# A transformer tower on one core: the last halving of the weighted pixels and the normalisation of the aggregate move from VectorE to GpSimd

## The chip, the core and the metric

The kernel runs on one core of a Trainium2 chip. A core has five engines, each with its own queue of instructions: TensorE (PE, matrix products and transposes), VectorE (DVE), ScalarE (ACT), GpSimd (POOL) and SyncE (SP), which issues the transfers here. Engines run side by side and hand work over by semaphores. Data lies in SBUF (128 partitions), matrix products arrive in PSUM. GpSimd reads and writes SBUF only in this kernel. The metric is the time of one execution on the device, in microseconds (us).

## The reference

Input `x` is (128, 64, 64, 64) in fp32: 128 images with 64 channels of 64x64 pixels. Three layers follow one another; the change lies in the first, the tokenizer:

```python
s = conv_stride                                   # 4
hw, n, d = (h * w, s * s, c // num_heads)         # 256 tokens, 16 pixels each, 8 channels a head
x = features.reshape(b, c, h, s, w, s)
reduce_feats = x.mean((3, 5)).reshape(b, c, hw).transpose(0, 2, 1)
unf = x.transpose(0, 1, 2, 4, 3, 5).reshape(b, c, hw, n).transpose(0, 2, 3, 1)
q = _ln(reduce_feats, ln_q_w, ln_q_b) @ Wq.T
kv = _ln(unf, ln_kv_w, ln_kv_b) @ Wkv.T
...
attn = jax.nn.softmax(jnp.einsum('bhpd,bhpnd->bhpn', q * scale, k), axis=-1)
aggre = jnp.einsum('bhpn,bhpnd->bhpd', attn, v)
return reduce_feats + aggre @ proj_w.T + proj_b
```

Each token looks at its own 16 pixels: a softmax over them, per head, and the weighted sum of their values. Behind it come a linear attention in chunks of 128 tokens with decay, a layer norm, a mixture of 8 experts of which 2 are taken, and a second layer norm:

```python
h = _layernorm(h + _L0_attn_ref(h, ...), axis=-1)
h = _layernorm(h + _L0_ffn_ref(h, ...), axis=-1)
```

## The kernel before

The program has two blocks. The first does the tokenizer, the linear attention and the first layer norm, and leaves its result in SBUF (`h1`); the second does the experts and stores. The change touches the first block only.

The first block works in 128 units. A unit is 128 tokens of each of two images, so `[128, 128]` tiles hold 128 tokens by two times 64 channels. Every engine has a function `step(i, r)`; step 4i + r of each engine works on several units at once, each at another stage: `there(i, r, lag)` asks whether unit 4i + r - lag exists, and `done(i, r, lag, per)` is the count of a semaphore when that unit's stage is through (`per` counts a unit). So the order of the work on an engine is the order in which its `step` is written, and what an instruction waits for is written before it. `units` runs ten steps of straight code at the start, then a loop of 29 passes with four steps in its body, then ten steps of straight code at the end. In the text, "the first step" to "the fourth step" are those of the loop's body; the first stands behind the loop's jump.

What happens around the change, for a unit u:

- One step after its keys and values, VectorE makes the softmax weights `aw` (128 tokens by 16 pixels by 16 heads of the two images) and `rden`, the reciprocal of the sum of the exponentials, at the end of the step.
- In the next step GpSimd multiplies the values `vs` by the weights, four products of 128x512 (L699), and folds the 16 pixels to 8 by two additions of 128x512 (L706), each in place in `pv`. In its queue there follow two parts of the attention of an older unit, `qm` (L713) and `htok` (L719), and the pixel sums of a unit two steps ahead, from `xb` by `xt` to `red` (L729 to L737).
- VectorE, behind the key product of its first quarter (`keys(0)`, L816), sums the 8 pixels that remain to `agg` by one reduction (L859) whose input is read with a stride of 128 elements, and multiplies by `rden` into `aggn` (L863). Then comes `keys(1)`, then three small instructions of a Newton step (L871 to L873) that wait for ScalarE's `y0s`, then the scaling of the queries `q` (L878) and `keys(2)`.
- TensorE, behind its `keys(1)`, transposes `aggn` (`aggregated`, L491), makes the second half of the values (L407), projects the turned aggregate (`projected`, L496) and goes on with `keys(2)` (L380, L385). ScalarE, between the two, adds a bias to the turned aggregate (`aggT`, L647), behind the squares of the centred input (`sqs`, L563) on its queue.

The key products form a chain of their own: TensorE writes quarter j into one bank of PSUM, VectorE multiplies it by the queries (`kqs`), and only then may TensorE write quarter j + 1.

## Time and profile before

| | |
|---|---|
| time, median of 3 runs | 2807.53 us (2804.64 to 2809.35) |
| the profiled execution | 2810.09 us, its span 2808.4 us |
| mean granted TensorE clock | 0.957 of full speed |
| TensorE busy | 2357.4 us (84%) |
| VectorE busy | 2050.6 us (73%) |
| ScalarE busy | 1907.3 us (68%) |
| GpSimd busy | 1785.9 us (64%) |

The first block takes some 2350 us of the span, the second the rest. Busy shares are averages: they tell which engine has room, and not what a step waits for. For that there are the waits (which engine stood idle, in front of which instruction, until whose work had ended) and the timeline, which lists instructions in order of time. Ends of matrix products are modelled, and GpSimd's spans are rough. In the rows, L699 is line 699 of the kernel.

### The profile page before, as it was taken

Reading aid. Unit: us, or ns where it says so; the run is one execution under the profiler, and the core shown is the slowest. Engines: PE = TensorE matmul, PEld = TensorE weight load, DVE = VectorE, ACT = ScalarE, POOL = GpSimd, SP = SyncE. Lnnn points to the kernel's source line nnn. Section 1 sums busy time; section 2 is a strip of 40 time slices with the busy share of each in tenths; the row PEclk is TensorE's granted clock in tenths of the full one; section 3 lists DMA queues with packets and bytes.
Section 4 is the critical chain, followed back from the end, with each engine's and each line's share of the span. In section 5 each row is a group of like instructions: output and inputs, shape, how many; then the busy total and the mean of one; then the engine's idle time right before and its main releaser. Section 6 shows DMA issues by size and latency. Waiting matters only on the chain. (4 is left out here: it accounts for less than half of the span.)

```text
span 2808.4 us, 93560 instructions
## 1 busy us (share of the span) xinstructions
PE 2357.4 (84%) x32965; PEld 1125.1 (40%) x32965; DVE 2050.6 (73%) x4680; ACT 1907.3 (68%) x4717; POOL 1785.9 (64%) x1821
## 2 busy tenths in 40 slices
PE   2788888888888888888888888888888886999997
PEld 1344444444444444444444444444444443333332
DVE  4677777777777777777777777777777776888887
ACT  3777777777777777777777777777777773555554
POOL 3677777777777777777777777777777763222323
PEclk9899999999999999999999999999999997999999
DMA  5333333222233333333323222333333300001001
GB/s 88 62 62 62 62 62 62 60 58 57 58 62 62 62 62 62 62 62 62 62 62 61 58 58 57 62 61 61 62 62 62 62 17 1 16 19 22 19 19 27
DMA packets 573761, 148.58 MB, mean 53 GB/s; under 512 B 573440, under 2 KB 573440, under 8 KB 573440
## 3 DMA queue, kind: packets, MB, share of 16 engines
q1 hardware_dynamic: 573440, 143.52, 25.7%
q8 instruction: 297, 4.87, 0.7%
q14 instruction: 24, 0.20, 0.0%
HBM read 135.09 MB, written 8.39 MB: 51 GB/s over the span
## 5 line engine op out<-in xcount | busy, mean ns | idle before, releaser
L699 POOL TENSOR_TENSOR pv<-vs,aw 128x512 f32<-128x512 f32 x512 | 535.3, 1078 | 565.8 <-DVE aw L916 565.8
L581 ACT ACTIVATE xd<-xb 128x512 f32<-128x512 f32 x512 | 573.6, 1146 | 0.0
L380 PE MATMUL ps<-xb,w_ckv 64*64 64x512 f32 x2048 | 553.4, 617 | 2.4 <-ACT sqs L563 1.9
L385 PE MATMUL ps<-xb,w_ckv 64*64 64x512 f32 x2048 | 553.4, 617 | 0.0
L816 DVE TENSOR_TENSOR kqs<-ps,qqT 128x512 f32<-128x512 f32 x512 | 351.3, 686 | 233.4 <-PE ps L385 231.3
L827 DVE TENSOR_TENSOR sm<-ps,decay 128x1024 f32<-128x1024 f32 x256 | 301.5, 1220 | 212.4 <-PE ps L462 212.4
L563 ACT ACTIVATE sqs<-ps 128x512 f32<-128x512 f32 x512 | 305.1, 596 | 87.7 <-PE ps L385 87.7
L570 ACT ACTIVATE vs<-ps 128x1024 f32<-128x1024 f32 x256 | 262.4, 1025 | 115.3 <-PE ps L407 112.4
L729 POOL TENSOR_TENSOR xt<-xb 128x512 f32<-128x512 f32 x256 | 326.1, 1297 | 21.6 <-issue 21.2
L706 POOL TENSOR_TENSOR pv<-pv 128x512 f32<-128x512 f32 x256 | 320.5, 1274 | 0.0
L859 DVE TENSOR_REDUCE agg<-pv 128x128 f32<-128x1024 f32 x128 | 253.2, 1978 | 77.9 <-POOL pv L706 77.9
L407 PE MATMUL ps<-w_ckv,xd 64*64 64x64 f32 x16384 | 298.9, 222 | 0.1
L407 PEld LDWEIGHTS ps<-w_ckv,xd 64*64 64x64 f32 x16384 | 264.5, 135 | 39.5 <-issue 16.9
L346 PE MATMUL ps<-kqs,selk 128*32 128x512 f32 x1024 | 161.6, 708 | 135.9 <-issue 76.8
L1217 ACT ACTIVATE hid<-ps,b1p 128x1024 f32<-128x1024 f32 x128 | 142.7, 1115 | 164.8 <-PE ps L1118 164.6
L1318 DVE TENSOR_TENSOR hid<-ps,hid 128x512 f32<-128x512 f32 x256 | 163.7, 685 | 25.1 <-PE ps L1130 13.3
L462 PE MATMUL ps<-qm,kT 32*128 32x512 f32 x1024 | 171.4, 744 | 0.0
L732 POOL TENSOR_TENSOR xt<-xt 128x512 f32<-128x512 f32 x128 | 162.6, 1270 | 10.0
L713 POOL TENSOR_TENSOR qm<-qT,hm 128x512 f32<-128x512 f32 x128 | 133.6, 1044 | 43.7 <-ACT kT L598 43.7
L349 PE MATMUL ps<-sqs,selv 128*32 128x512 f32 x1024 | 159.7, 700 | 0.0
L597 ACT ACTIVATE qT<-ps 128x128 f32<-128x128 f32 x128 | 35.5, 278 | 170.1 <-PE ps L437 170.1
L475 PEld LDWEIGHTS ps<-sm,vpad 128*32 128x32 f32 x4096 | 104.1, 109 | 108.0 <-issue 101.5
(213 smaller groups left out, 4455.6 us busy)
## 6 DMA issues: line engine op xcount, KB each, us to landing
xb<-in_x_dram SPq DMA_DIRECT2D x512, 256.0 KB, 4.3
out_dram<-outb SPq DMA_DIRECT2D x128, 64.0 KB, 1.6
w1p<-in_L_ffn_w_dram SPq DMA_DIRECT2D x16, 16.0 KB
w2p<-in_L_ffn_w_dram SPq DMA_DIRECT2D x8, 16.0 KB
b1p<-in_L_ffn_b_dram SPq DMA_DIRECT2D x8, 0.2 KB
sm<-in_L_tok_Wkv_dram SPq DMA_DIRECT2D x4, 16.0 KB, 2.0
w_av<-in_L_attn_w_qkv_dram SPq DMA_DIRECT2D x4, 16.0 KB, 2.1
b2v<-in_L_ffn_b_dram SPq DMA_DIRECT2D x4, 2.0 KB
```

Source lines behind the costliest of these rows:

```text
L380: nc.tensor.matmul(KB[own, :], w_ckv[own, 2 * P + m * C:2 * P + (m + 1) * C], xv[own, j], start=True, stop=True)
L385: mm = nc.tensor.matmul(CB[(1 - m) * C:(2 - m) * C, :], w_ckv[own, m * C:(m + 1) * C], xv[own, j], start=True, stop=True)
L407: mm = nc.tensor.matmul(VB[m][h * C:(h + 1) * C, n * C:(n + 1) * C], xv[own, d, b, h * C:(h + 1) * C], w_ckv[own, P + m * C:P + (m + 1) * ...
L563: nc.scalar.activation(sqs[:, j, :], CB, ACT.Square).then_inc(cs_done, 1)
L570: nc.scalar.activation(vs[:, s, v * 8 * P:(v + 1) * 8 * P].rearrange("p (n m c) -> p m n c", m=2, c=C), ps[:, 2:4, :].rearrange("p m (n c) ...
L581: nc.scalar.activation(xd[:, j, :].rearrange("p (b t) -> p b t", b=ST), xb[:, f, :].rearrange("p (b t d) -> p d b t", b=ST, d=ST)[:, j], A ...
L699: nc.gpsimd.tensor_tensor(pv[:, at].rearrange("p (k d) -> p k d", d=D), vs[:, s, at].rearrange("p (k d) -> p k d", d=D), aw[:, j * W4:(j + ...
L706: nc.gpsimd.tensor_tensor(pv[:, j * 4 * P:(j + 1) * 4 * P], pv[:, j * 4 * P:(j + 1) * 4 * P], pv[:, (j + 2) * 4 * P:(j + 3) * 4 * P], ALU. ...
L729: ins = nc.gpsimd.tensor_tensor(xt[:, h * H:(h + 1) * H], xb[:, f, h * H:(h + 1) * H], xb[:, f, (h + 2) * H:(h + 3) * H], ALU.add)
L816: V.tensor_tensor(kqs[:, j, :].rearrange("p (t d) -> p t d", d=ST), KB.rearrange("p (t d) -> p t d", d=ST), qqT[:, s, :].unsqueeze(2).to_b ...
L827: V.tensor_tensor(sm[:, f * 1024:(f + 1) * 1024].rearrange("p (h c) -> p h c", c=P), ps[:, 2 * f:2 * f + 2, :].rearrange("p g (h c) -> p ( ...
L859: V.tensor_reduce(agg[:], pv[:, 0:8 * P].rearrange("p (n c) -> p c n", c=P), AX, ALU.add).then_inc(agg_ch, 1)
```

## The change

Three things. GpSimd makes a third addition of 128x512 behind its two, which folds 8 pixels to 4, under a new semaphore `pv_half`; `pv_done` now counts this one. VectorE's reduction reads 4 pixels (512 elements of a partition) in place of 8. The multiplication by `rden` leaves VectorE and stands on GpSimd, behind `htok` and ahead of the pixel sums, with the same two waits. Two waits are new on VectorE: the reduction waits until GpSimd has read the `agg` of the unit before, and the reciprocal waits until GpSimd has read `rden`.

```diff
--- before.py
+++ after.py
@@ -218,6 +218,7 @@
             ex_done = sem("ex_done")
             aw_done = sem("aw_done")
             pv_ch = sem("pv_ch")
+            pv_half = sem("pv_half")
             pv_done = sem("pv_done")
             agg_ch = sem("agg_ch")
             agg_done = sem("agg_done")
@@ -705,7 +706,10 @@
                             pool.wait_ge(pv_ch, done(i, r, 2, ST, j - 1))
                             nc.gpsimd.tensor_tensor(pv[:, j * 4 * P:(j + 1) * 4 * P], pv[:, j * 4 * P:(j + 1) * 4 * P],
                                                     pv[:, (j + 2) * 4 * P:(j + 3) * 4 * P],
-                                                    ALU.add).then_inc(pv_done, 1)
+                                                    ALU.add).then_inc(pv_half, 1)
+                        pool.wait_ge(pv_half, done(i, r, 2, 2))
+                        nc.gpsimd.tensor_tensor(pv[:, 0:4 * P], pv[:, 0:4 * P], pv[:, 4 * P:8 * P],
+                                                ALU.add).then_inc(pv_done, 1)
                     if there(i, r, 3):
 
                         pool.wait_ge(qk_ev, done(i, r, 3, 2))
@@ -718,6 +722,14 @@
                         pool.wait_ge(vk_ev, done(i, r, 3, 2))
                         nc.gpsimd.tensor_tensor(htok[:, o, :], htok[:, o, :], bp_row[:],
                                                 ALU.add).then_inc(hb_done, 1)
+                    if there(i, r, 2):
+
+                        pool.wait_ge(agg_ch, done(i, r, 2, 1))
+                        pool.wait_ge(agT_pe, done(i, r, 3, 1))
+                        nc.gpsimd.tensor_tensor(aggn[:].rearrange("p (j d) -> p j d", d=D),
+                                                agg[:].rearrange("p (j d) -> p j d", d=D),
+                                                rden[:].unsqueeze(2).to_broadcast([P, SL, D]),
+                                                ALU.mult).then_inc(agg_done, 1)
                     if there(i, r, -2):
 
                         f = (r + 2) % 4
@@ -855,14 +867,10 @@
                     keys(0)
                     if there(i, r, 2):
 
-                        dve.wait_ge(pv_done, done(i, r, 2, 2))
-                        V.tensor_reduce(agg[:], pv[:, 0:8 * P].rearrange("p (n c) -> p c n", c=P), AX,
+                        dve.wait_ge(pv_done, done(i, r, 2, 1))
+                        dve.wait_ge(agg_done, done(i, r, 3, 1))
+                        V.tensor_reduce(agg[:], pv[:, 0:4 * P].rearrange("p (n c) -> p c n", c=P), AX,
                                         ALU.add).then_inc(agg_ch, 1)
-                        dve.wait_ge(agg_ch, done(i, r, 2, 1))
-                        dve.wait_ge(agT_pe, done(i, r, 3, 1))
-                        V.tensor_tensor(aggn[:].rearrange("p (j d) -> p j d", d=D),
-                                        agg[:].rearrange("p (j d) -> p j d", d=D),
-                                        rden[:].unsqueeze(2).to_broadcast([P, SL, D]), ALU.mult).then_inc(agg_done, 1)
                     keys(1)
 
                     link, n = chain(dve, newt_ch, (4 * i + r + 2) * 3)
@@ -917,6 +925,7 @@
                                         ALU.mult).then_inc(aw_done, 1)
                         V.tensor_reduce(den[:], sn.rearrange("p n j -> p j n"), AX, ALU.add).then_inc(den_done, 1)
                         dve.wait_ge(den_done, done(i, r, 1, 1))
+                        dve.wait_ge(agg_done, done(i, r, 2, 1))
                         link(V.reciprocal(rden[:], den[:]))
                         assert n[0] == 5
                 units(dve, step)
```

GpSimd's queue, in the second step of the loop's body, from the products to the pixel sums; before:

```order
L699 TENSOR_TENSOR pv<-vs,aw 128x512 x4
L705 REGISTER_ALU
L706 TENSOR_TENSOR pv<-pv 128x512 x2
L712 REGISTER_ALU
L713 TENSOR_TENSOR qm<-qT,hm 128x512
L719 TENSOR_TENSOR htok<-htok,bp_row 128x128
L727 REGISTER_ALU
L729 TENSOR_TENSOR xt<-xb 128x512 x2
```

The same place in the changed kernel, whose lines lie further down (`hm` is the mask of the heads, REGISTER_ALU computes a count that is waited for):

```order
L700 TENSOR_TENSOR pv<-vs,aw 128x512 x4
L706 REGISTER_ALU
L707 TENSOR_TENSOR pv<-pv 128x512 x2
L711 TENSOR_TENSOR pv<-pv 128x512
L716 REGISTER_ALU
L717 TENSOR_TENSOR qm<-qT,hm 128x512
L723 TENSOR_TENSOR htok<-htok,bp_row 128x128
L729 TENSOR_TENSOR aggn<-agg,rden 128x128
L739 REGISTER_ALU
L741 TENSOR_TENSOR xt<-xb 128x512 x2
```

Everything behind the products has moved down by one instruction, and the pixel sums by two; `aggn` has `qm` and `htok` between itself and the addition on which it depends by way of VectorE.

VectorE's queue from `keys(0)` to the Newton step, again in the second step of the loop's body, before and then after, with the semaphores that each row waits for:

```order
L816 TENSOR_TENSOR kqs<-ps,qqT 128x512 [waits sel_pe,qq_done,kc_pe]
L859 TENSOR_REDUCE agg<-pv 128x128 [waits pv_done]
L863 TENSOR_TENSOR aggn<-agg,rden 128x128 [waits agT_pe,agg_ch]
L812 REGISTER_ALU
L816 TENSOR_TENSOR kqs<-ps,qqT 128x512 [waits kc_pe]
```

After:

```order
L828 TENSOR_TENSOR kqs<-ps,qqT 128x512 [waits sel_pe,qq_done,kc_pe]
L872 TENSOR_REDUCE agg<-pv 128x128 [waits agg_done,pv_done]
L824 REGISTER_ALU
L828 TENSOR_TENSOR kqs<-ps,qqT 128x512 [waits kc_pe]
L877 ISA
L879 SCALAR_TENSOR_TENSOR ps<-ps,y0s 128x16x3 [waits rs_ch]
```

One instruction is gone between the two key products, and the second follows the reduction. The queues of TensorE, ScalarE and SyncE are as they were.

## Rows read from the trace of the kernel before

**Rows 1.** The page: busy us, share of the span, instructions.
```profile
PE 2357.4 (84%) x32965; PEld 1125.1 (40%) x32965; DVE 2050.6 (73%) x4680; ACT 1907.3 (68%) x4717; POOL 1785.9 (64%) x1821
```
**Rows 2.** Groups by line: count, busy us, mean ns, idle us before and its releaser.
```profile
L699 POOL TENSOR_TENSOR pv<-vs,aw 128x512 f32<-128x512 f32 x512 | 535.3, 1078 | 565.8 <-DVE aw L916 565.8
...
L706 POOL TENSOR_TENSOR pv<-pv 128x512 f32<-128x512 f32 x256 | 320.5, 1274 | 0.0
...
L859 DVE TENSOR_REDUCE agg<-pv 128x128 f32<-128x1024 f32 x128 | 253.2, 1978 | 77.9 <-POOL pv L706 77.9
...
L719 POOL TENSOR_TENSOR htok<-htok,bp_row 128x128 f32<-128x128 f32 x128 | 58.8, 460 | 1.7
...
L1327 DVE TENSOR_REDUCE nst<-y 128x8 f32<-128x512 f32 x32 | 21.6, 676 | 5.0 <-POOL y L1052 5.0
...
L1286 DVE TENSOR_REDUCE top<-rest 128x8 f32<-128x64 f32 x32 | 7.0, 220 | 1.1
```
**Rows 3.** One line, the normalisation: duration in ns, least, median, greatest.
```profile
L863 DVE TENSOR_TENSOR aggn<-agg,rden x128: 291/746/1157, 86.6 to 2341.5; 128x128 f32<-128x128 f32 x128
```
**Rows 4.** Waits from 1000 to 1200 us: us in total, times, longest us.
```profile
PE ps L491 <- DVE aggn L863: 5.2, 9, 0.7
...
DVE ps L871 <- ACT y0s L642: 3.7, 8, 0.7
PE ps L496 <- ACT aggT L647: 3.4, 9, 0.4
...
PE ps L491 <- ACT l L556: 1.0, 2, 0.5
```
**Rows 5.** Timeline, a third step: start us, us, instruction, count [idle before, releaser].
```profile
1004.92 0.42 DVE L916 TENSOR_TENSOR aw<-ps,yrs 128x256 f32<-128x256 f32 x1
...
1005.50 4.18 POOL L699 TENSOR_TENSOR pv<-vs,aw 128x512 f32<-128x512 f32 x4 [3.92 <-DVE aw L916]
...
1009.64 2.52 POOL L706 TENSOR_TENSOR pv<-pv 128x512 f32<-128x512 f32 x2
...
1012.10 1.05 POOL L713 TENSOR_TENSOR qm<-qT,hm 128x512 f32<-128x512 f32 x1
1012.19 1.97 DVE L859 TENSOR_REDUCE agg<-pv 128x128 f32<-128x1024 f32 x1 [0.70 <-POOL pv L706]
...
1013.10 0.47 POOL L719 TENSOR_TENSOR htok<-htok,bp_row 128x128 f32<-128x128 f32 x1
...
1014.20 0.75 DVE L863 TENSOR_TENSOR aggn<-agg,rden 128x128 f32<-128x128 f32 x1
...
1015.05 0.30 PE L491 MATMUL ps<-ident,aggn 128*128 128x128 f32 x1 [0.68 <-DVE aggn L863]
...
1015.28 1.16 PE L407 MATMUL ps<-w_ckv,xd 64*64 64x64 f32 x64
...
1016.04 0.36 ACT L647 ACTIVATE aggT<-ps,bv_col 128x128 f32<-128x128 f32 x1
...
1016.43 1.22 DVE L878 TENSOR_SCALAR q<-qps,yrs 128x64 f32<-128x64 f32 x2
...
1016.55 0.46 PE L496 MATMUL ps<-aggT,w_pj 128*128 128x128 f32 x2
...
1018.10 0.69 DVE L816 TENSOR_TENSOR kqs<-ps,qqT 128x512 f32<-128x512 f32 x1 [0.45 <-PE ps L385]
```
**Rows 6.** Timeline, the first step behind the jump.
```profile
1049.32 1.97 DVE L859 TENSOR_REDUCE agg<-pv 128x128 f32<-128x1024 f32 x1
...
1051.04 1.27 POOL L732 TENSOR_TENSOR xt<-xt 128x512 f32<-128x512 f32 x1
...
1051.33 1.13 DVE L863 TENSOR_TENSOR aggn<-agg,rden 128x128 f32<-128x128 f32 x1
...
1054.38 0.46 PE L496 MATMUL ps<-aggT,w_pj 128*128 128x128 f32 x2 [0.40 <-ACT aggT L647]
```
**Rows 7.** Timeline of TensorE, a fourth step.
```profile
1031.77 0.30 PE L491 MATMUL ps<-ident,aggn 128*128 128x128 f32 x1 [0.47 <-DVE aggn L863]
...
1033.49 0.46 PE L496 MATMUL ps<-aggT,w_pj 128*128 128x128 f32 x2 [0.32 <-ACT aggT L647]
```

## The prediction

> **What bounds the kernel now.** I read the busy shares first. No engine is full: TensorE is busy 84% of the span, VectorE 73%, GpSimd 64% [rows 1]. So the shares don't decide it, and the question is which wait ends last around the aggregate. The groups by line come next: VectorE's reduction of eight pixels takes 1.98 us, 128 times [rows 2], and its normalisation 0.29 to 1.16 us, median 0.75 [rows 3]. That is 2.7 us of VectorE in each step, and it looks like much. The waits of a steady stretch correct this [rows 4]: of 11 steps, TensorE's transpose of the aggregate waits for VectorE in 9 and for ScalarE in 2, but the projection two places later on the same queue waits again, for ScalarE, in 9.
>
> The timeline of one step, the third of the four in the loop's body, shows why [rows 5]. GpSimd multiplies from 1005.50 and adds to 1012.16. VectorE reduces from 1012.19 to 1014.17 and normalises to 1014.95, and TensorE transposes at 1015.05. The values follow until 1016.44. The projection starts at 1016.55. Its other input, `aggT`, was ready on ScalarE at 1016.40, and ScalarE had reached it late: it began at 1016.04, 0.69 behind the transpose's end, since queries, squares and the logarithm chain stand ahead of it on that queue. So ScalarE fixes the projection at 0.15 us behind `aggT`, and the aggregate only has to be in time. How much in time? Work that queues up on TensorE starts 0.07 us ahead of the modelled end of what precedes it (the values at 1015.28, the transpose's end at 1015.35), so the projection could have started at 1016.37: 0.18 us of slack. In the fourth step TensorE idles 0.32 us before the projection, in the first 0.40 [rows 6, 7], and over three steps of four 0.38 on average (3.4 us in 9 waits [rows 4]), so in the second like the first; with the same 0.07 the slack is 0.39, 0.47 and 0.47.
>
> **The change part by part.** Third addition on GpSimd: 128x512, as the two before it, 1.27 us [rows 2], behind a wait on GpSimd's own semaphore. In the third step it begins at about 12.24 (0.08 for that wait is my estimate) and ends at 13.51 (I write 12.24 for 1012.24). Behind it queue `qm` (1.05) and `htok` (0.47), which overlap their predecessor by 0.05 each: `qm` to 14.50, `htok` to 14.92 [rows 5]. Only then comes the new multiplication.
>
> Reduction of four pixels on VectorE: not in the trace. From below: the reduction of 512 adjacent elements took 0.68 us [rows 2]. From above: 1978 ns for 1024 is 0.76 more than the adjacent pace would give (a fixed 0.155 plus 1.02 ns an element, fitted through 512 elements and the 220 ns of 64 [rows 2]); if that surplus belongs to the 128 outputs and not to the elements, 512 cost 0.155 + 0.52 + 0.76 = 1.44 us. I take 1.07: fixed part 0.155, the rest halved, since the reads alone keep their stride. It then runs 13.54 to 14.61, and GpSimd hears of it 0.16 later (VectorE's `aw` ends at 5.34, GpSimd starts at 5.50 [rows 5]): 14.77. The multiplication isn't waiting for it, because its queue is busy until 14.92. That holds for any reduction up to 1.2 us.
>
> The normalisation on GpSimd: not in the trace either. Its nearest form is the 128x512 product with a broadcast factor, 1078 ns; `htok` (460 ns for 128) and the additions (1274 ns for 512) split into 189 ns fixed and 2.12 ns an element [rows 2]. A quarter of 889 plus 189 is 0.41. Bounds: 0.29, the shortest on VectorE [rows 3], and 0.46, `htok`. From 14.87 it ends at 15.28, and TensorE starts 0.10 later as before: 15.38 in place of 15.05. So the transpose is 0.33 late in the third step, 0.18 of it is slack, and 0.15 us is lost. In the fourth step the same sum (0.31 to 0.33 late, slack 0.39) gives nothing. In the second it was ScalarE that the transpose waited for [rows 4], so it is late by less than 0.33, with 0.47 of slack: nothing. In the first step GpSimd is early (VectorE reduces long after the additions, 1049.32 [rows 6]); the product is there by 1050.9, before the old one began, and the transpose could go earlier, but ScalarE's chain keeps the projection at 1054.38: no gain.
>
> Sum: the third step's pattern occurs 31 times (29 passes of the loop and two units outside): 31 x 0.15 = 4.6 us. In the last two units nothing covers the chain: 1.35 more for the addition (with its wait), 0.83 less for the reduction, and the product on GpSimd instead of VectorE with its signal, 0.3, make about 0.8 each; TensorE's other work hides most of the first, so 1.0. Together 5.6 us on a profiled execution of 2810.1 us. That one lies 2.6 above the median of the runs, 2807.5, and so the forecast is 2813.
>
> What VectorE gains, 1.98 - 1.07 + 0.75 = 1.66 us a step, I cost at nothing. The key product after it starts about 0.3 earlier, but then the Newton step waits for ScalarE's `y0s`, in 8 of 11 steps already before [rows 4].
>
> GpSimd gets 1.27 + 0.41 us a step more. Its sums of the next but one unit (`xt`, `red`) move by 1.7 us in three steps and by 2.4 in the first. It idles 4.4 us a step on average before the next weights (565.8 us in 128 waits [rows 2]), and 3.92 before this one [rows 5], and `red` is read only in the next step, so this is covered. The new wait of VectorE before the reciprocal asks for a product that was finished 6 us before.
>
> **A rule against the change.** VectorE's normalisation takes 0.75 us here and 1.13 where a GpSimd addition has just begun: 1051.33 to 1052.46, with the addition of 1051.04 ending at 1052.31 [rows 6], while its shortest is 0.29. It stands still until GpSimd's instruction ends. The Trainium skill, GPSIMD Engine Reference (Key points), says that GpSimd shares its SBUF interfaces with VectorE and that VectorE instructions with two SBUF inputs contend: the trace agrees. The same page (Engine selection) says not to put elementwise work on GpSimd, about twice as slow for two inputs. By that alone the move would lose; by this trace it replaces 0.75 with an estimated 0.41, since the contention goes with it. The Trainium skill, VectorE: DVE Perf Modes (the perf-mode tier table), gives a reduction one element a cycle, which would make the new one as short as the lower bound; the 1.98 us of the old one speak against it, and the sum would stay the same.
>
> **Rivals.** (1) Slower clearly: the reduction costs per output. Place: the product on GpSimd then waits for VectorE. Price at 1.44 us: third step 13.54 + 1.44 + 0.16 = 15.14, transpose 15.65, 0.60 late, 0.42 lost; fourth step 0.60 late, 0.21 lost; others nothing. 0.63 x 30 = 19 us, with the ends 2828. It decides from 1.2 us on. For it: the halving is only argued. Against it: the surplus goes with the one property that the adjacent reductions lack, the stride, which acts on every element read. A late signal or a slow start on GpSimd would act at the same place in the same way, with 0.1 us costing 3 us, and up to 6 once the fourth step is reached.
>
> (2) Collision: the scaling of the queries (`q`) is a VectorE instruction that today waits for GpSimd's addition, 1.22 us for the pair at 1016.43 [rows 5]. With GpSimd 1.7 us later it meets the two back-to-back additions from `xb`. The first goes through at their boundary at 16.5, the second may stand until 17.8. The next key product starts at 18.10 today, waiting for TensorE. So it costs nothing unless the second falls behind a further addition, to 19.1: then about 0.9 us in one kind of step, 26 us, 2834.
>
> (3) Faster: VectorE sets the pace by its key products, and 0.3 us a step come back in three steps of four: 96 x 0.26 = 25 us, 2782. Against it are the waits for ScalarE and TensorE named above. Smaller and likelier: the first step after the loop's jump varies by a microsecond from pass to pass, and another layout in time may take 0.2 us of it, 6 us.
>
> **How the numbers follow.** A run of this kernel can be told from no change at 0.2%, 5.6 us. The forecast, a small loss of 2 to 8 us, has 0.65; its own range is 2809 to 2816. Rival 1 with late signals has 0.20, rival 2 has 0.06, rival 3 with the jump 0.09. The forecast lies on the bound, so its chance splits: 0.43 within 0.2% and 0.22 slower. With the rivals: slower 0.47 (0.22 + 0.20 + 0.05), same 0.44, faster 0.09. The range reaches down to 2806, which leaves out most of rival 3, and up to 2828, the end of rival 1.
>
> **What would show it.** The transpose about 0.45 us behind `htok`'s end in the third step, and TensorE's wait before the projection gone there; the same wait down to under 0.1 in the fourth, untouched in the second. The reduction near 1.07 us. GpSimd's idle time before the weights down by 1.7 us a step. I am wrong if the reduction is over 1.2 us, if GpSimd starts the product later than `htok` lets it, or if the Newton step after the key product starts earlier than ScalarE's `y0s` allows today.

## The result, and the profile after

The changed kernel takes 2832.61 us (median of 4 runs, 2828.81 to 2833.62) against 2808.44 for the kernel before on the same chip: a ratio of 1.010, 95% interval 1.0072 to 1.0128. The forecast was 2813, its range 2806 to 2828, so the result lies 4.6 us outside. The profiled execution took 2828.81 us, its span 2827.1, which is 18.7 more than before.

The page of the kernel after, busy us of each engine, answers to [rows 1]:

```profile
PE 2346.5 (83%) x32965; PEld 1125.2 (40%) x32965; DVE 1875.7 (66%) x4552; ACT 1911.0 (68%) x4717; POOL 1986.0 (70%) x2077
```

VectorE has 175 us less, GpSimd 200 more. The groups by line of the same kernel answer to [rows 2, 3]:

```profile
L700 POOL TENSOR_TENSOR pv<-vs,aw 128x512 f32<-128x512 f32 x512 | 535.0, 1076 | 354.6 <-DVE aw L924 354.6
...
L872 DVE TENSOR_REDUCE agg<-pv 128x128 f32<-128x512 f32 x128 | 136.2, 1064 | 208.3 <-POOL pv L711 208.3
...
L711 POOL TENSOR_TENSOR pv<-pv 128x512 f32<-128x512 f32 x128 | 162.6, 1270 | 10.0
...
L729 POOL TENSOR_TENSOR aggn<-agg,rden 128x128 f32<-128x128 f32 x128 | 51.8, 404 | 33.7 <-DVE agg L872 33.7
```

The new operations cost what was forecast: the reduction 1.06 us (1.07), the product 0.40 (0.41), the addition 1.27, and GpSimd's idle time before the weights fell from 565.8 to 354.6 us, 1.65 a step (1.7). A third step of the kernel after, in the timeline, answers to [rows 5]; brackets are idle time before an instruction and its releaser:

```profile
1008.99 1.27 POOL L711 TENSOR_TENSOR pv<-pv 128x512 f32<-128x512 f32 x1
...
1010.29 1.06 DVE L872 TENSOR_REDUCE agg<-pv 128x128 f32<-128x512 f32 x1 [2.03 <-POOL pv L711]
...
1011.22 0.45 POOL L723 TENSOR_TENSOR htok<-htok,bp_row 128x128 f32<-128x128 f32 x1
...
1011.63 0.40 POOL L729 TENSOR_TENSOR aggn<-agg,rden 128x128 f32<-128x128 f32 x1
...
1012.14 0.30 PE L492 MATMUL ps<-ident,aggn 128*128 128x128 f32 x1 [1.05 <-POOL aggn L729]
...
1013.19 1.52 DVE L886 TENSOR_SCALAR q<-qps,yrs 128x64 f32<-128x64 f32 x2
...
1013.46 0.49 PE L497 MATMUL ps<-aggT,w_pj 128*128 128x128 f32 x2
...
1013.59 1.02 ACT L571 ACTIVATE vs<-ps 128x1024 f32<-128x1024 f32 x1 [0.42 <-PE ps L408]
...
1015.03 0.69 DVE L828 TENSOR_TENSOR kqs<-ps,qqT 128x512 f32<-128x512 f32 x1 [0.32 <-PE ps L386]
...
1016.23 0.30 PE L431 MATMUL ps<-ident,q 128*128 128x128 f32 x1 [0.85 <-DVE kqs L828]
```

The product stands right behind `htok`, TensorE's transpose 0.47 us behind `htok`'s end, and the projection follows the values directly. All this is as forecast. Two things are not, and the same step of the kernel before shows them:

```profile
1016.50 1.02 ACT L570 ACTIVATE vs<-ps 128x1024 f32<-128x1024 f32 x1
...
1019.14 0.30 PE L430 MATMUL ps<-ident,q 128*128 128x128 f32 x1 [0.69 <-DVE kqs L816]
```

ScalarE's copy of the values' second half (L571 after, L570 before) waits 0.42 us for TensorE, where before it followed `aggT` without a wait. TensorE turns the queries (L431, before L430) 2.77 us after the projection's start in place of 2.59, which is 0.18 us later. The waits of TensorE and ScalarE over the whole loop, 230 to 2240 us (us in total, times, longest), of before:

```profile
PE ps L346 <- issue: 76.8, 28, 3.1
PE ps L430 <- DVE kqs L816: 61.2, 113, 0.7
...
PE ps L496 <- ACT aggT L647: 31.6, 84, 0.4
...
ACT vs L570 <- PE ps L407: 97.2, 112, 0.9
```

and of after:

```profile
PE ps L347 <- issue: 76.3, 28, 3.2
PE ps L431 <- DVE kqs L828: 75.8, 113, 0.9
...
PE ps L497 <- ACT aggT L648: 19.6, 56, 0.4
...
ACT vs L571 <- PE ps L408: 116.6, 171, 0.9
```

The copy waits 59 times more, about once in each third and each fourth step, and the turning of the queries waits 14.6 us longer in sum. The projection lost its wait in 28 steps: these are the fourth ones, where the forecast had left it under 0.1 us.

I measured each step from projection to projection, mean over the loop; an interval bears the name of the step whose projection ends it. What an engine does behind a step's projection therefore falls into the next interval: the third step's copy of the values and its turning of the queries lie in the fourth interval. Third: 16.575 us before, 16.716 after. Fourth: 16.949 and 17.129. First, the one that holds the loop's jump: 21.018 and 20.293. Second: 17.011 and 17.008. With 29, 29, 28 and 28 of them the loop's part is +4.1, +5.2, -20.3 and -0.1 us; the units ahead of the steady part give +0.9 and those behind it +4.4; the second block gives +24.5. Up to rounding that makes the 18.7.

So two surprises outweigh everything that the forecast argued about. The first is the shorter first step. Each line is one such step: its start and end, its length, the busy time of PE, PEld, DVE, ACT and POOL, and then TensorE's granted clock as a share of full speed (0.84 in the first line), ahead of the DMA share. Of before:

```profile
1033.49:1054.38 20.89, 16.73 (x240) 7.58 (x241) 13.12 (x27) 12.85 (x34) 14.71 (x16) 0.84 0.27 53
1104.90:1126.03 21.13, 16.75 (x241) 7.60 (x241) 13.14 (x27) 12.87 (x34) 14.74 (x16) 0.84 0.25 53
```

and of after:

```profile
1030.58:1050.99 20.41, 15.70 (x242) 7.43 (x241) 11.58 (x26) 13.10 (x34) 16.49 (x17) 0.92 0.25 54
1101.84:1120.54 18.70, 14.05 (x240) 7.19 (x241) 11.68 (x26) 13.12 (x34) 15.96 (x17) 1.00 0.29 60
```

At 0.84 TensorE ran at the lower level (1.2 GHz) for (1 - 0.84) x 2 x 20.9 = 6.7 us of the step, at 0.92 for half of that, at 1.00 never; it fell after TensorE's idle time at the jump. Before, 26 of 28 passes were of the first kind; after, 4 were, 20 of the second kind and 4 of the third. In sum over the loop the lower level holds for 184 us before and 96 after, while TensorE's wait at the jump itself is the same (76.8 and 76.3 us).

The second surprise is in code that the change doesn't touch. VectorE in the second block, 2536 to 2542 us, after:

```profile
2538.34 0.17 DVE L1310 TENSOR_SCALAR top<-top 128x8 f32<-128x8 f32 x1 [2.59 <-issue]
2540.60 0.17 DVE L1311 TENSOR_SCALAR top<-top 128x8 f32<-128x8 f32 x1 [2.09 <-issue]
2540.81 0.23 DVE L1312 TENSOR_TENSOR ra<-ra,top 128x64 f32<-128x64 f32 x1
```

The same three in the kernel before:

```profile
2534.31 0.40 DVE L1301 TENSOR_SCALAR top<-top 128x8 f32<-128x8 f32 x1
2534.74 0.52 DVE L1302 TENSOR_SCALAR top<-top 128x8 f32<-128x8 f32 x1
2535.30 0.23 DVE L1303 TENSOR_TENSOR ra<-ra,top 128x64 f32<-128x64 f32 x1
```

They are the first instructions behind the jump of the second block's loop. "issue" means a wait for nothing that the profile shows. It occurs in all five passes that begin with the jump back, twice in each, 22.3 us in sum, and in the kernel before it never occurs. The pages' part on DMA queues counts the packets of the instruction queues (packets, MB, share); after:

```profile
q8 instruction: 292, 4.78, 0.7%
q14 instruction: 50, 0.41, 0.0%
```

and before:

```profile
q8 instruction: 297, 4.87, 0.7%
q14 instruction: 24, 0.20, 0.0%
```

One queue fetched twice as many packets.

The waits and the 24.5 us are not quite the same thing. In the eleven kernels below that have no such waits the second block takes 466.2 to 469.2 us, and this goes with its own time at the lower clock level (35.6 to 49.2 us) at about 0.2 us for each us. In the changed kernel that time is 78.1 us (before 35.9), with one stretch right after each of the five pairs of waits. By the same slope, extrapolated, some 8 us of the 24.5 come with the clock and 16 from the waits themselves; this split is my estimate.

The Trainium skill, Runtime: NRT & Kernel Launch (Instruction fetch mechanics), says that instructions are fetched in blocks of 256, that most engines hold two of them and TensorE more, and that a taken branch whose target is in neither forces a fetch before execution goes on. The change takes three instructions out of VectorE's program ahead of that loop: its 323 instructions start at number 963 before and at 960 after. If a block begins between the two, the loop lies in two blocks before and in three after. The following runs test that first.

### The profile page after: what moved, and what is told of

It is laid out like the page before. It is cut to its first block and busy times, and to the rows that moved or that the text cites. A ratio compares the mean times of both kernels' runs of the same rounds, so it can differ in the third digit from the quotient of the medians.

```text
span 2827.1 us, 93857 instructions
## 1 busy us (share of the span) xinstructions
PE 2346.5 (83%) x32965; PEld 1125.2 (40%) x32965; DVE 1875.7 (66%) x4552; ACT 1911.0 (68%) x4717; POOL 1986.0 (70%) x2077
## 5 line engine op out<-in xcount | busy, mean ns | idle before, releaser
L700 POOL TENSOR_TENSOR pv<-vs,aw 128x512 f32<-128x512 f32 x512 | 535.0, 1076 | 354.6 <-DVE aw L924 354.6
L571 ACT ACTIVATE vs<-ps 128x1024 f32<-128x1024 f32 x256 | 262.1, 1024 | 132.2 <-PE ps L408 132.2
L741 POOL TENSOR_TENSOR xt<-xb 128x512 f32<-128x512 f32 x256 | 319.7, 1269 | 21.5 <-issue 21.0
L707 POOL TENSOR_TENSOR pv<-pv 128x512 f32<-128x512 f32 x256 | 320.6, 1274 | 0.0
L872 DVE TENSOR_REDUCE agg<-pv 128x128 f32<-128x512 f32 x128 | 136.2, 1064 | 208.3 <-POOL pv L711 208.3
L347 PE MATMUL ps<-kqs,selk 128*32 128x512 f32 x1024 | 150.3, 660 | 134.2 <-issue 76.3
L711 POOL TENSOR_TENSOR pv<-pv 128x512 f32<-128x512 f32 x128 | 162.6, 1270 | 10.0
L463 PE MATMUL ps<-qm,kT 32*128 32x512 f32 x1024 | 161.0, 701 | 0.0
L1050 POOL TENSOR_TENSOR outb<-y,yrs 128x512 f32<-128x512 f32 x32 | 33.4, 1042 | 177.0 <-DVE yrs L1347 177.0
L1127 PE MATMUL ps<-tokT,w1p 64*128 64x512 f32 x512 | 150.0, 664 | 0.0
```

What stands on the lines that cost most here:

```text
L571: nc.scalar.activation(vs[:, s, v * 8 * P:(v + 1) * 8 * P].rearrange("p (n m c) -> p m n c", m=2, c=C), ps[:, 2:4, :].rearrange("p m (n c) ...
L700: nc.gpsimd.tensor_tensor(pv[:, at].rearrange("p (k d) -> p k d", d=D), vs[:, s, at].rearrange("p (k d) -> p k d", d=D), aw[:, j * W4:(j + ...
L707: nc.gpsimd.tensor_tensor(pv[:, j * 4 * P:(j + 1) * 4 * P], pv[:, j * 4 * P:(j + 1) * 4 * P], pv[:, (j + 2) * 4 * P:(j + 3) * 4 * P], ALU. ...
L741: ins = nc.gpsimd.tensor_tensor(xt[:, h * H:(h + 1) * H], xb[:, f, h * H:(h + 1) * H], xb[:, f, (h + 2) * H:(h + 3) * H], ALU.add)
L1127: mm = nc.tensor.matmul(UB[p % 2][:, m, :], w1p[h, p, :], tokT[h, (r + ahead) % 4, :], start=True, stop=True)
```

## The experiments

Each kernel was timed in rounds together with the kernel before, whose median was 2811.03 us beside e1 to e4, 2809.27 beside e5 to e8 and 2812.21 beside e9 to e12; the ratio compares within these rounds. The steps are the mean intervals as above; "low" is the time at the lower clock level in the loop, "second block" the time from the last transpose of an aggregate to the end (us). All of these come from one profiled execution. The last column has the mean granted clock of that execution and, behind it, the median over all executions of the kernel: where the two differ, as in e3, e4, e6 and e9, the profiled one is not typical in its low time.

| kernel | ratio (95%) | third | fourth | first | second step | low | second block | clock |
|---|---|---|---|---|---|---|---|---|
| before | 1 | 16.575 | 16.949 | 21.018 | 17.011 | 184 | 466.5 | 0.957, 0.956 |
| after | 1.010 (1.0072-1.0128) | 16.716 | 17.129 | 20.293 | 17.008 | 96 | 491.1 | 0.965, 0.964 |
| e1 | 1.0023 (1.0009-1.0037) | 16.717 | 17.131 | 20.529 | 17.012 | 120 | 468.2 | 0.966, 0.965 |
| e2 | 1.007 (1.0045-1.0095) | 16.571 | 16.938 | 21.107 | 17.004 | 188 | 487.3 | 0.951, 0.953 |
| e3 | 1.0016 (0.9999-1.0034) | 16.568 | 17.053 | 20.678 | 17.005 | 150 | 466.9 | 0.961, 0.957 |
| e4 | 0.9971 (0.9956-0.9986) | 16.569 | 16.778 | 21.197 | 17.015 | 157 | 469.2 | 0.959, 0.965 |
| e5 | 0.9992 (0.998-1.0005) | 16.724 | 16.811 | 20.765 | 17.007 | 123 | 467.5 | 0.963, 0.966 |
| e6 | 0.9988 (0.9971-1.0004) | 16.569 | 17.072 | 20.291 | 17.004 | 116 | 466.2 | 0.967, 0.962 |
| e7 | 0.9969 (0.9952-0.9987) | 16.574 | 17.085 | 20.380 | 17.008 | 126 | 467.7 | 0.966, 0.965 |
| e8 | 0.9968 (0.9952-0.9985) | 16.574 | 16.782 | 21.090 | 17.008 | 147 | 466.4 | 0.963, 0.962 |
| e9 | 0.9978 (0.9962-0.9993) | 16.577 | 16.783 | 20.781 | 17.011 | 126 | 468.5 | 0.967, 0.963 |
| e10 | 0.9975 (0.9962-0.9989) | 16.571 | 16.779 | 21.224 | 17.008 | 154 | 469.0 | 0.960, 0.961 |
| e11 | 0.9964 (0.9942-0.9987) | 16.870 | 16.948 | 19.876 | 17.011 | 96 | 469.0 | 0.969, 0.967 |
| e12 | 1.0112 (1.0094-1.013) | 16.730 | 17.133 | 20.645 | 17.012 | 130 | 476.1 | 0.965, 0.966 |

**e1: the changed kernel, VectorE's loop back at 963.**

```diff
                 link(V.memset(eps_c[:], EPS))
+                link(V.memset(eps_c[:], EPS))
+                link(V.memset(eps_c[:], EPS))
+                link(V.memset(eps_c[:], EPS))
```

> The changed kernel with three more instructions of VectorE, all in its setup (the memset of one constant, repeated), so that the loop of the second block stands where it stood before the change: 963 instructions from the start of VectorE's program instead of 960. Nothing else differs. Theory F (VectorE's instructions have to be fetched at the second block's jump): the ten waits for issue of 2.0 to 2.6 us in front of the two first share instructions go away, the stretch from the first block's last transpose of the aggregate to the end of the span falls from 491 to 467 us, and the kernel takes 2832 - 22 = about 2808 us, no change against before (0.998 to 1.002). Rival G (the second block is longer because of the TensorE clock or the state in which the first leaves it): the stretch stays at 485 to 495 us and the time at 2830 to 2834.

2816.78 us (2809.51 to 2824.41). The waits for issue are gone and the second block is 23 us shorter. Three added instructions took about three quarters of the loss away. What is left, 1.0023, lies just outside the 0.998 to 1.002 that was expected. In its profiled execution, 4.2 us longer than that of before, the third step stands at +4.1 us over the loop, the fourth at +5.3, the first at -13.7, the units ahead of the steady part and behind it at +6.9 and the second block at +1.7.

**e2: the kernel before, its loop moved to 960.** Three memsets of the setup go from VectorE to GpSimd, and nothing else changes.

```diff
+                nc.gpsimd.memset(ssq[:], 1.0).then_inc(s_zero, 1)
+                nc.gpsimd.memset(eps_c[:], EPS).then_inc(s_zero, 1)
...
-                link(V.memset(ssq[:], 1.0))
-                link(V.memset(eps_c[:], EPS))
...
-                link(V.memset(selk[:], 0.0))
```

(`selk` joins the loop of GpSimd's memsets, whose count of waits grows by three.)

> The kernel before, with three memsets of VectorE's setup made by GpSimd, so that VectorE's second loop stands at instruction 960, as in the changed kernel. The aggregate is computed as before. Theory F: ten waits for issue of 2.0 to 2.6 us appear in front of the two first share instructions, and the kernel takes 20 to 24 us more than before, 1.007 to 1.009. Rival G: same as before, within 0.2%.

2831.9 us (2821.06 to 2834.46). The waits appear without any part of the change; VectorE's waits from 2400 us on:

```profile
DVE top L1300 <- issue: 11.2, 5, 2.3
DVE top L1301 <- issue: 10.4, 5, 2.1
```

**e12: the loop at 1163.** If blocks of 256 are the reason, a place can be named where the waits come back: one begins between 961 and 963, so others begin near 1218 and 1474, and a loop from 1163 to 1485 lies in three.

```diff
+                link(V.memset(eps_c[:], EPS))
```

This line stands there 203 times more. These memsets make the setup some 18 us longer than in e1, so the total says nothing here; the waits and the second block do.

> The changed kernel with 203 small VectorE memsets in the setup, so that VectorE's second loop (323 instructions) starts at its instruction 1163 (same output). Starts at 963 (three kernels) had no waits at that loop's jump, starts at 960 (two kernels) two a pass. Page theory: VectorE's instructions come in pages of 256, one begins at 961 to 963, so the next ones at 1217 and 1473; a loop from 1163 to 1485 needs three pages where one from 963 needs two, and waits for `issue` of 2 to 2.6 us come back at its jump, one or two a pass in 5 of 6 passes, 10 to 25 us in all, the second block at 478 to 492 us. Rival: only a start just ahead of a page is bad, or the earlier padding helped for another reason: no such waits, second block at 467. The memsets themselves cost 10 to 30 us of setup, which is not part of the question.

One wait in each of the same five passes, at the jump's target; the second one is missing, since from 1163 the next block is some 55 instructions away and not one to three. The waits of VectorE from 2400 us on, and the fetches:

```profile
DVE top L1513 <- issue: 11.9, 5, 2.6
```

```profile
q14 instruction: 52, 0.43, 0.1%
```

The kernels with the loop at 963 have 24 to 26 packets on this queue, e2 has 49. The second block takes 476.1 us, 7 to 10 more than in the kernels at 963, though 2 less than the 478 to 492 that was expected: with the slope of the clock as above, 8 us for 11.9 us of waits, and in e2 16 for 21.6. With e1 and e2 this settles the cause: the place of the loop in VectorE's program, not the work of the change. The rule of the Trainium skill agrees with these three starts; what a fetch costs it does not say; the waits here are 2.0 to 2.6 us long. That a block begins between 961 and 963 is my inference from the two starts; no run names a block's border directly.

**e3: third addition and reduction of four, normalisation left on VectorE; e4: normalisation on GpSimd, the reduction over eight.** Both with the loop at 963. e3 takes from the change these two pieces:

```diff
+                        nc.gpsimd.tensor_tensor(pv[:, 0:4 * P], pv[:, 0:4 * P], pv[:, 4 * P:8 * P],
+                                                ALU.add).then_inc(pv_done, 1)
...
-                        V.tensor_reduce(agg[:], pv[:, 0:8 * P].rearrange("p (n c) -> p c n", c=P), AX,
+                        V.tensor_reduce(agg[:], pv[:, 0:4 * P].rearrange("p (n c) -> p c n", c=P), AX,
```

and e4 this one, with its waits:

```diff
-                        V.tensor_tensor(aggn[:].rearrange("p (j d) -> p j d", d=D),
+                        nc.gpsimd.tensor_tensor(aggn[:].rearrange("p (j d) -> p j d", d=D),
```

> Only the third addition on GpSimd and the reduction of four pixels; the normalisation stays on VectorE. VectorE's second loop is put at instruction 963. In the third step of the pass the reduction runs from 13.54 to 14.61 on the scale of the rows of before, and the normalisation then stands still behind GpSimd's instruction (htok to 14.92, then the sums): 14.9 to 15.1 if it passes at that boundary. Theory A (the aggregate is late on TensorE, and ScalarE's copy of the values with it): transpose 0.0 to 0.2 us late, third step plus fourth step 0 to 0.2 us longer than before instead of 0.32. First block within 5 us of before at the same share of the low clock; total 0.998 to 1.003. Rival (contention): the normalisation waits for the first sum from xb, to 16.2, the transpose is 1.1 us late, and each pass loses 1 us or more: 2840.

> Only the normalisation on GpSimd; GpSimd makes two additions and VectorE reduces eight pixels. VectorE's second loop is put at instruction 963. GpSimd's htok is through at 13.57, the reduction at 14.17, so the product runs 14.30 to 14.71 and the transpose starts at 14.81 in the third step, 0.24 us earlier than before. Theory A: ScalarE binds the projection, so the third step is no shorter than before by more than 0.05 us, the others the same, and the total within 0.3% of before. Rival (the aggregate bound TensorE before): each of three steps 0.2 us shorter, 96 x 0.2 = 19 us, 0.993.

e3 took 2816.53 us, which its interval does not tell from no change, and e4 2800.78, a gain of 0.29%. The third addition costs 0.10 us in the fourth step; the normalisation on GpSimd takes 0.17 off it, where no change had been expected. Together they cost 0.14 in the third and 0.18 in the fourth, more than the parts: there the product stands behind GpSimd's longer queue. e4's profiled execution (2812.42) was the slowest of its runs, with the lowest clock, so where its gain arises can't be read from it; what goes with the gain stands behind e10 below.

**e5: on ScalarE the gather ahead of the values' copy.**

```diff
+                    gather(0)
                     values(1)
-                    gather(0)
                     centred(2)
```

> The changed kernel with its VectorE loop back at instruction 963, and on ScalarE the gather of the next unit's first plane ahead of the copy of the values' second half (two lines exchange places; the output is the same). Theory A: the fourth step loses 0.18 us since ScalarE's copy now waits for the values and drags the gather, the squares of the third plane, and so TensorE's turning of the queries behind it. With the gather first it fills that wait: the fourth step comes back to 16.95 +- 0.05 us from 17.13, the third stays at 16.72 (its projection waits for the transpose itself), and the time is 0.18 x 31 = 5 us below the 2816.8 of the aligned changed kernel if TensorE's clock at the jump stays as it was there. Rival B: the fourth step loses at the projection, because the transpose is later than the slack allows: then it stays at 17.13 and the time within 3 us of 2817. Rival C: the copy made 0.5 us later by the gather delays the products that read the values: steps longer by 0.1 to 0.3 us, 2820 to 2830.

The fourth step takes 16.811 us in place of 17.131, the third 16.724 as foretold: a loss of 0.18 turned into a gain of 0.14, more than the 0.18 that I had given it. ScalarE's waits over the loop:

```profile
ACT vs L571 <- PE ps L408: 98.0, 113, 0.9
```

The 59 new waits are gone, and those left are the copy of the first half, as before. So the fourth interval lost at that copy, the third step's own, and at what queues behind it (gather, squares of the third plane, turning of the queries), not at the projection. The copies of the fourth steps wait in the same way and fall into the first interval, where the clock hides what they cost.

**e6: the product ahead of `htok` on GpSimd.** The two exchange places, with their waits.

```diff
-                        nc.gpsimd.tensor_tensor(htok[:, o, :], htok[:, o, :], bp_row[:],
-                                                ALU.add).then_inc(hb_done, 1)
...
                         nc.gpsimd.tensor_tensor(aggn[:].rearrange("p (j d) -> p j d", d=D),
...
+                        nc.gpsimd.tensor_tensor(htok[:, o, :], htok[:, o, :], bp_row[:],
+                                                ALU.add).then_inc(hb_done, 1)
```

> The changed kernel with its VectorE loop at instruction 963, and on GpSimd the normalisation ahead of the addition of `htok` and not behind it (same output). The reduction ends 0.28 us before the normalisation starts today, 0.16 of which the signal needs, so the transpose should come 0.12 us earlier. Theory A (everything lost in the third and fourth step hangs on the transpose): third step 16.72 to 16.60, fourth 17.13 to 17.01, and 0.24 x 30 = 7 us less than the 2816.8 of the aligned changed kernel, 2810, at the same clock; less if TensorE's low clock at the jump lasts longer again. Rival: the later `htok` (0.4 us) is itself needed by TensorE or VectorE in the next step: no gain or a loss of up to 3 us.

The third step takes 16.569 us, which takes back the whole 0.15, a little more than expected. The fourth takes 17.072, which is 0.06 less and not the 0.12 expected: ScalarE's copy still waits 142 times, some 30 more than in the kernel before, all of them in third steps. The product now waits for the reduction itself, as the timeline of a third step shows:

```profile
1004.31 1.03 POOL L717 TENSOR_TENSOR qm<-qT,hm 128x512 f32<-128x512 f32 x1
1005.52 0.41 POOL L725 TENSOR_TENSOR aggn<-agg,rden 128x128 f32<-128x128 f32 x1 [0.18 <-DVE agg L876]
1005.89 0.45 POOL L732 TENSOR_TENSOR htok<-htok,bp_row 128x128 f32<-128x128 f32 x1
```

**e7: a small delay in the kernel before**, in the third and fourth steps of the loop's body.

```diff
+                    if r >= 2 and there(i, r, 0):
+                        nc.scalar.activation(l2[:, 0:C], ident[:, 0:C], ACT.Copy)
                     centred(2)
```

> The kernel before with one small extra ScalarE copy (about 0.24 us, into a scratch tile that is overwritten later; same output) ahead of the squares of the third plane in the third and fourth steps of the loop. It makes those steps later without any part of the change. Clock theory: a small delay in these steps changes how long TensorE stays at 1.2 GHz behind the jump (184 us in the loop of the kernel before, 96 to 150 in those with the third addition), so the low stretches should shorten to 90 to 160 us, the first step drop from 21.02 to 20.3 to 20.8, and the whole lie 0 to 5 us above the kernel before although third and fourth steps grow by 0.1 to 0.25 us each (3 to 14 us in sum). Rival: the third addition or the less busy VectorE shortens the low stretch, not the delay: low clock stays near 184 us, the first step at 21.0, and the time rises by the full growth of the steps, 5 to 14 us, to 2816 to 2824.

Pure extra work made the kernel 0.31% faster, which is beyond even what the clock theory gave. The copies fall behind their steps' projections, so they lie in the fourth and the first interval. The fourth grew by 0.14, the first fell by 0.64 in spite of its copy, and 14 of 28 passes had the long stretch at the lower level in place of 26. The third interval did not grow, against the expectation.

**e11: the delay in another step.** The kernel before with two copies where `r == 1`.

```diff
+                    if r == 1 and there(i, r, 0):
+                        nc.scalar.activation(l2[:, 0:C], ident[:, 0:C], ACT.Copy)
+                        nc.scalar.activation(l2[:, C:2 * C], ident[:, 0:C], ACT.Copy)
                     centred(2)
```

The copies fall behind that step's projection, so the interval of the third step grows, by 0.30.

> The kernel before with two small extra ScalarE copies (0.5 us) ahead of the squares of the third plane in the second step of the loop and none in the others (same output). Tells whether a shorter low clock needs a delay just ahead of the jump, or only another length of the pass. If the place matters: second step 17.01 to 17.2, first still 21.0 with about 184 us of low clock, 0 to 6 us slower than before. If it is the length of the pass: low clock falls to 90 to 150 us as soon as the pass changes by 0.1 us or more, first step 20.3 to 20.8, time 2795 to 2812. If ScalarE's slack hides the copies, all steps as before.

The ratio is 0.9964, the first step takes 19.876 us, and the lower level holds for 96 us, as much as in the changed kernel. Three of its first steps:

```profile
951.77:971.89 20.12, 15.69 (x241) 7.49 (x241) 13.14 (x27) 12.84 (x34) 14.75 (x16) 0.92 0.28 55
1022.66:1041.17 18.51, 14.05 (x240) 7.19 (x241) 12.89 (x27) 12.85 (x34) 14.43 (x16) 1.00 0.27 59
1091.95:1112.28 20.33, 15.69 (x240) 7.51 (x241) 13.13 (x27) 12.85 (x34) 14.74 (x16) 0.92 0.25 54
```

The delay need not be near the jump. What the first step gains in the changed kernel needs neither less VectorE work nor the third addition: a kernel with neither gets it.

**e8: e4 with e5's exchange. e10: e8 with e7's copy where `r == 3` alone. e9: the exchanges of e5 and e6 together.**

```diff
+                    if r == 3 and there(i, r, 0):
+                        nc.scalar.activation(l2[:, 0:C], ident[:, 0:C], ACT.Copy)
```

> Only the normalisation on GpSimd (the reduction still sums eight pixels), the VectorE loop at instruction 963, and the gather ahead of the copy of the values' second half (same output). Theory A: normalisation alone gave 2800.8 with the fourth step at 16.78; the copy hardly waits for the values there, so the exchange is worth 0 to 0.1 us a step, 2797 to 2801. If the copy is what the fourth step waits for even there, up to 0.15 us x 60, 2792. Rival C: the values' copy 0.5 us later costs: 2803 to 2812.

> Normalisation alone on GpSimd with the gather first (16.574 / 16.782 / 21.090 / 17.008 us for the four steps, 147 us of low clock, ratio 0.9968), and now one small extra ScalarE copy ahead of the squares of the third plane in the fourth step (same output). Clock theory: the fourth step grows by 0.1 to 0.25 us and the first falls by 0.3 to 0.7 us as in the delayed kernel before, with low clock at 90 to 130 us: ratio 0.993 to 0.997. If what that delay did was particular to the kernel before: first step stays at 21.1, ratio 0.998 to 1.0.

> The changed kernel with its VectorE loop at instruction 963, the normalisation ahead of the `htok` addition on GpSimd, and the gather ahead of the copy of the values' second half on ScalarE (same output). If the two losses are separate, as the earlier runs say, the third step is 16.57 (as with the product ahead) and the fourth 16.75 to 16.82 (as with the gather first), and the whole is 8 to 10 us under the aligned changed kernel's 1.0023 of the kernel before, 0.9985 to 0.999, by those alone; TensorE's low clock behind the jump decides the rest: at 120 us of it, 2800 to 2806, at 180 us, 2806 to 2812. If the two repair the same wait, the fourth step stays over 16.95.

e8 equals e4 within the intervals. In e10 the copy falls behind the fourth step's projection, so its own interval is the first, which grew by 0.13; the low clock did not shorten (147 to 154 us), and the ratio is 0.9975. The clock theory had the first step fall by 0.3 to 0.7: a miss. It doesn't undo e7 and e11, but shows that not every delay helps. e9 hit both steps, 16.577 and 16.783, and with 0.9978 makes of the whole change a small gain.

That this and the other gains belong to the changes is not shown, though. The mean granted clock is on record for every execution. Over the 93 of the kernel before that were timed beside e1 to e12 it runs from 0.950 to 0.963, and the time goes with it, from 2823.8 us at the lowest to 2794.5 at the highest: some 20 us for 0.01 of clock. Every kernel that came out faster by more than its interval (e4, e7 to e11) has a higher median clock than before, by 0.005 to 0.011. At that rate this is worth 10 to 22 us (an estimate, as it carries the slope over to other kernels), while they gained 5 to 12. So the clock alone could account for each of these gains, and in e4 the steps don't: over the loop the fourth steps gain 5.0 us, while the wait at the jump, below, grows by 19.8.

Another wait shows in the kernels with a fourth step of 16.8 us (e4, e5, e8, e9, e10). TensorE's waits at the jump, over the whole loop, in e4:

```profile
PE ps L346 <- issue: 96.6, 28, 4.6
```

and e5:

```profile
PE ps L347 <- issue: 94.3, 28, 4.3
```

against 76.8 before. In 11 and 12 passes it is over 3.8 us, and queue q8 fetches 310 and 318 packets, not 297. Where the fourth step gains 0.17 us, the wait at the jump grows by 0.71 (19.8 us / 28); e4's first step is 0.18 longer than before in spite of less low clock. That a fetch takes longer there is suggested by the packets, but no run tried it.

## Why the prediction was wrong

**The sum stopped at the first block.** It went through 31 third steps and the last two units, and held all other code at its old time without saying so. That term, put at nothing without a reason, is the step that failed: no step names the second block, and there 24.5 us arose, more than the 19.6 by which the time exceeds the forecast. The runs showed in its place two waits at each jump back of VectorE's second loop, 22.3 us in sum, which come and go with the loop's start at 960 or 963 (after and e2 against e1 and before). None of the signs that the prediction named for being wrong could have shown it, since all lay in the first block. Rival 2's 2834 is close to the measured 2832.6 by chance; its mechanism is not what happened. With the shift undone (e1) the ratio is 1.0023, which on 2807.5 is 2814 beside the forecast's 2813.

**That agreement is luck.** In e1 the third and fourth steps and the units at both ends lost 16.3 us where the forecast had 5.6, and the first step gave 13.7 back. "In the fourth step the same sum gives nothing" was right for the projection, which starts there without a wait, and wrong for the interval: it grew by 0.18 us, 5.2 in sum. Slack was measured at the projection alone (0.18 us in the third step, 0.39 in the fourth), but TensorE's values stand between transpose and projection, and a later transpose also makes their second half late, for which ScalarE's copy had next to no slack (e5). The third step's 0.15 was right in size (0.14). Its cause was right too as far as e6 shows, which took it back by an earlier product.

**The ends were mis-sized**: 1.0 for the last two units, measured 4.4, since five of the last six intervals grew and not two. In the sum itself, 0.83 for the shorter reduction should be 0.91 by its own 1.98 and 1.07, and the surplus of the strided reduction is 0.78 and not 0.76; neither changes the forecast.

**"No gain" for the first step failed the other way**, by -20 us. Rival 3 had named a gain of 0.2 us from the jump; it was 0.7. e7 and e11 show that it comes with the clock and that a change without any use can bring it; e10 shows that not every one does.

**Right**: the prices of the three operations, the product behind `htok` and not waiting for the reduction (it waits only in first steps, 24 of 28), that GpSimd has room for its later sums, VectorE's 1.66 us a step worth nothing, the untouched second step. The Newton step after the key product waits for ScalarE in 11 of 11 steps where it was 8 [rows 4]; the waits of after from 1000 to 1200 us:

```profile
DVE ps L879 <- ACT y0s L643: 6.7, 11, 0.7
```

Rival 1 did not happen: the reduction takes 1.06 us for half the elements and the same outputs, so most of its cost goes with the elements. Rival 2's collision may be there, as the `q` pair takes 1.52 us in place of 1.22, but its end at 1014.71 is ahead of the key product at 1015.03. The rule that elementwise work is slow on GpSimd did not decide: the product takes 0.40 us there against a median of 0.75 on VectorE [rows 3], and alone (e4) it shortens the fourth step by 0.17 us.

**Open**: what decides in a pass how long TensorE stays at 1.2 GHz. The loop of before was profiled twice (184, 188 us in before and e2), the changed one three times (96, 120, 130 in after, e1 and e12), and the medians of the clock agree: 0.956 for before against 0.964 to 0.966 for these three. So kernels differ. But executions differ too: the twelve of e7 run from 0.956 to 0.968, 2816.5 to 2791.1 us. e10 shows that not every addition changes it.

## What to carry to other kernels

Removing or adding a few instructions on an engine with more than one loop shifts every later loop of that engine: count from the start of its program where each loop begins, before and after, and look for new waits for issue at jumps in code that the change does not touch. When a result is late by some tenths, take the slack of everything that queues behind it on the same engine, not only of its direct reader. And where a loop's jump drops TensorE's clock, a gain or loss of a few tenths of a per cent has to be compared with what a useless delay does to the same kernel, and with the granted clock of every execution, before it is credited to the change.

## What the runs showed of the hardware

- VectorE's jump back into a loop of 323 instructions was followed by waits of 2.0 to 2.6 us: two a pass with the loop's start at instruction 960 (after, e2), one at 1163 (e12), none at 963.
- TensorE's wait at its loop's jump, 2.7 us on average, grows to 3.4 where the fourth step is 0.14 to 0.17 us shorter, with 13 to 21 more packets (e4 and e5) on the instruction queue q8.
- 0.5 us of useless ScalarE work in a pass of 71.55 us went with a pass of 70.71, as TensorE spent 96 us in place of 184 at 1.2 GHz behind the jump (e11).
- In 93 executions of the kernel before, 0.01 of mean granted clock went with 20 us of 2811.
- A strided reduction of 128x512 into 128 outputs took 1064 ns and of 128x1024 1978 ns [rows 2]: 1.8 ns for each further element, where adjacent elements take 1.0 by the fit of the prediction.
